# Routing weights computed earlier in the round, and a residual sum moved from GpSimd to VectorE, in a graph-attention and expert-network kernel

## The reference

```python
x = x + gnn0(layernorm(x), adj)      # masked softmax attention, then ELU
x = x + ffn0(layernorm(x), ...)      # router picks 2 of 6 experts per node
x = x + gnn1(layernorm(x), adj)      # masked softmax attention, then ELU
x = x + ...                          # one choice of 2 of 8 experts per graph, layernorm
# inside ffn0, per node:
rh = relu(features @ router_w1 + router_b1)
expert_logits = softmax(rh @ router_w2 + router_b2)
top_w, top_i = top_k(expert_logits, 2)
routing_weights = softmax(top_w)
```

## Time and profile before

| | |
|---|---|
| Time, median of 3 runs | 764.93 us (764.13 to 765.67) |
| Time of the profiled execution | 764.48 us |
| Its span | 762.7 us |
| Instructions | 15258 |
| TensorE busy | 607.0 us (80%) |
| VectorE busy | 448.5 us (59%) |
| ScalarE busy | 408.3 us (54%) |
| GpSimd busy | 253.4 us (33%) |

### The profile page before, as it was taken

One profiled execution on the slowest core, in us unless ns is written; L12 is line 12 of the kernel. 1 busy time (PEld: TensorE's weight loads), 2 busy tenths in 40 slices (PEclk: granted clock), 3 DMA queues, 4 the chain that ended last, 5 costly groups with the idle time before them and its releaser, 6 DMA issues.

```text
span 762.7 us, 15258 instructions
## 1 busy us (share of the span) xinstructions
PE 607.0 (80%) x3969; PEld 489.7 (64%) x4001; DVE 448.5 (59%) x1632; ACT 408.3 (54%) x974; POOL 253.4 (33%) x477
## 2 busy tenths in 40 slices
PE   3358779797887978879797797968942699999993
PEld 2236566575665756657575575746631599999993
DVE  3356576686866768677576766765533144444445
ACT  1234455664755658456575665746641255555552
POOL 4312222341423324233232423322221034444444
PEclk9999999998998999899899989999955699999997
DMA  7304214034040320404214041121100454444421
GB/s 155 104 2 125 85 41 126 28 99 119 8 124 11 113 99 26 124 1 124 74 51 124 0 124 46 38 84 30 57 0 0 133 146 139 140 142 142 142 69 55
DMA packets 74598, 61.99 MB, mean 81 GB/s; under 512 B 7772, under 2 KB 62268, under 8 KB 74562
## 3 DMA queue, kind: packets, MB, share of 16 engines
q1 hardware_dynamic: 61344, 56.14, 24.6%
q10 hardware_dynamic: 13218, 5.42, 2.8%
HBM read 57.13 MB, written 4.41 MB: 81 GB/s over the span
## 4 chain that ended last, share of the span: by engine, by line
PE 65%; DVE 12%; ACT 9%; issue 8%; POOL 4%; DMA 1%; ACTq 0%; DVEq 0%; POOLq 0%; SPq 0%
PE bank L1297 13%; PE bank L1310 9%; PE bank L1474 4%; PE wide L240 4%; PE bank L1487 4%; PE wide L207 4%; PE wide L1487 4%; PE wide L1474 3%; DVE at_lk L300 3%; PE bank L1289 3%; PE bank L1290 3%; PE bank L1291 3%; PE wide L232 2%; ACT h L787 2%; ACT h L782 2%
## 5 line engine op out<-in xcount | busy, mean ns | idle before, releaser
L782 ACT ACTIVATE h<-bank,b 128x512 f32<-128x512 f32 x96 | 65.9, 687 | 125.6 <-PE bank L1297 125.3
L1297 PE MATMUL bank<-h,w 128*128 128x512 f32 x192 | 114.3, 680 | 5.1 <-ACT h L787 5.1
L1310 PE MATMUL bank<-w,h2w 128*128 128x128 f32 x768 | 109.6, 288 | 0.0
L1310 PEld LDWEIGHTS bank<-w,h2w 128*128 128x128 f32 x768 | 102.6, 204 | 4.3 <-issue 1.0
L996 DVE TENSOR_TENSOR h2w<-h,wide_w 128x512 f32<-128x512 f32 x96 | 65.6, 683 | 44.3 <-ACT h L782 43.3
L787 ACT ACTIVATE h<-bank,b 128x512 f32<-128x512 f32 x96 | 65.4, 681 | 41.4 <-PE bank L1291 41.2
L1289 PE MATMUL bank<-xnTh,w1h 128*128 128x512 f32 x96 | 76.6, 798 | 0.0
L1316 PE MATMUL wide<-ident,wgt 128*88 128x128 f32 x16 | 6.3, 393 | 72.7 <-DVE wgt L1053 72.7
L324 POOL TENSOR_TENSOR at_src<-at_wh,zero 128x8 bf16<-128x8 f32 x32 | 9.0, 280 | 128.9 <-DVE at_wh L292 128.9
L1316 PEld LDWEIGHTS wide<-ident,wgt 128*88 128x88 f32 x16 | 2.2, 138 | 76.6 <-DVE wgt L1053 76.6
L101 POOL TENSOR_TENSOR at_var_eps<-at_mean_var,eps 128x4 f32<-128x4 f32 x32 | 12.3, 385 | 108.0 <-DVE at_mean_var L94 108.0
(11 more groups left out here) (233 smaller groups left out, 1526.5 us busy)
## 6 DMA issues: line engine op xcount, KB each, us to landing
wide_w<-w_scratch SPq DMA_DIRECT2D x96, 256.0 KB, 4.3
mask<-in_L_ffn_W SPq DMA_DIRECT2D x128, 128.0 KB, 2.1
x<-in_x SPq DMA_DIRECT2D x16, 256.0 KB, 5.9
xin<-in_x SPq DMA_DIRECT2D x16, 256.0 KB, 6.0
adj_in<-in_adj SPq DMA_DIRECT2D x16, 256.0 KB, 6.3
out<-at_pr ACTq DMA_DIRECT2D x8, 256.0 KB, 3.0
out<-at_prT ACTq DMA_DIRECT2D x8, 256.0 KB, 2.7
W<-in_L_ffn_W SPq DMA_DIRECT2D x2, 512.0 KB
```

The costliest lines, as they stand in the source:

```text
L782: a.activation(h2[:, e % 2, :], b_h2[:, :], ACT.Relu, bias=b2[:, e:e + 1]).then_inc(h2_ready, 1)
L1297: pe.matmul(b_h2[:, :], w2[:, e, :], h1[:, e % 2, :], start=True, stop=True).then_inc(l2_done, 1)
L1310: last = pe.matmul(b_out[:, s], h2w[:, e % 2, s], w3[:, e, :], start=False, stop=(e == E0 - 1), skip_group_check=True)
```

## The change

Two things are moved and one changes its engine. The exponential `pq` goes, on ScalarE, from behind the second attention's score copy to a place ahead of `norm_apply_act`. `route_weights` goes, on VectorE, from behind `measure(rn)` to a place ahead of `attn_dve_elu(at0)`; `weight_rows`, its neighbour so far, stays. The residual sum of the first attention is taken from GpSimd and is done by VectorE right behind that ELU, as one operation on 128x512 elements of fp32, both inputs in SBUF. No transfer and no matrix product moves.

```diff
--- before.py
+++ after.py
@@ gpsimd @@
-                if live("attn0", i0):
-                    attn_pool_residual(at0, p, x, x[:, cols(i + 2)], const_ready, i + 2)
@@ scalar @@
                 if attn1:
                     attn_act_rows(at1, a, i - 1)
+                if route:
+                    a.wait_ge(route_step, ROUTE * (i + 1) + 7)
+                    a.activation(pq[:, :, :], pd[:, :, :], ACT.Exp).then_inc(pq_ready, 1)
                 if pool and not last(i0):
...
                     attn_act_z(at1, a, i - 1)
-                if route:
-                    a.wait_ge(route_step, ROUTE * (i + 1) + 7)
-                    a.activation(pq[:, :, :], pd[:, :, :], ACT.Exp).then_inc(pq_ready, 1)
@@ vector @@
                     weigh(n + 3, i, 3)
+                if route:
+                    route_weights(i + 1)
                 if attn0:
                     attn_dve_elu(at0, v, i + 2)
+                    settle(v, const_ready)
+                    v.wait_ge(at0["elu_ready"], i + 3)
+                    v.tensor_tensor(x[:, cols(i + 2)], x[:, cols(i + 2)], at0["prT"][:, :], ALU.add)\
+                        .then_inc(at0["x_ready"], 1)
                 if run:
                     weigh(n + 4, i, 4)
...
                 if route:
-                    route_weights(i + 1)
                     weight_rows(i + 1)
```

## The result

The changed kernel took 671.4 us, the median of 4 runs (668.54 to 673.78), against 765.3 us (764.13 to 766.58) for the kernel before: a ratio of 0.877, with an interval of 0.873 to 0.881. The prediction said 669.0 us. The execution in the trace took 673.78 us and is the slowest of the four. The prediction's sum, worked out from the profiled execution of the kernel before, was 668.4 us, so this execution lies 5.4 us above it.

What follows compares the result with a forecast made beforehand. TensorE was taken to set the pace, stopped once a round by VectorE's `wgt`. Twelve rounds gave 76.6 us, with the other rounds 96.1, off 764.5: 668.4, so 669 us; range 659 to 688, the forecast's own 663 to 675.

Steps and rivals of the forecast that it cites:

- The wait and its place: TensorE's 4.66 us wait for `wgt` ahead of the weights' transpose goes entirely, with 1.4 us to spare.
- The clock: On TensorE behind the wait, the granted clock of 0.52 goes; it and what hangs on it give 1.7 us per round.
- the rival that only the wait goes: TensorE still stands somewhere long enough for the slow clock; 1.5 us in 13 rounds come back, 688 us, chance 0.05.
- L300 and the residual: On VectorE the residual costs 0.69 us plus 0.05 of wait, while L300 falls from 1.75 to 0.69 us.
- What is late next: The exponential L269 on ScalarE becomes the close second; TensorE stands 0.1 to 0.4 us for it, round 25.83 us.
- the term of 76.6 us: The gain in the loop: 12 rounds, each shorter by 6.38 us.
- The terms for round 0 (5.7 us): Round 0 gains 4.42 us of wait and some 1.3 us of clock.
- what lies behind the 12 rounds (8.0): Gains of 6.2 us in round 13's second half and 1.8 us in round 14.
- The transfers: VectorE waits about 0.5 us for `x`, absorbed by 0.74 us of later idle time; nothing charged, upper bound 0.47 us.
- the loop of transfers binds: Rival: the loop from `wrow` through loads, `x`, statistics and weighings limits the rounds; 675 us, or 687, chance 0.14.
- a wait of over 0.5 us per round at `x`: Sign named beforehand: such a wait, at `x` or at `wide_w`, would make the forecast number too low.
- The prologue and round 0: Round -1 gains 5.0 us of wait without clock; round -2 gains 0.8 us from the residual moving to VectorE.

Runs made afterwards that it cites:

- e6: The changed kernel with the exponential `pq` back at its old place on ScalarE, VectorE's new order kept: 702.2 us, ratio 0.918.
- e2: The changed kernel with the first attention's residual given back to GpSimd, only the weights staying moved: 675.5 us, ratio 0.881.
- e7: The kernel before, with 36 unread transposes of a constant put on TensorE ahead of the weights' transpose: 742.3 us, ratio 0.969.
- e1: The changed kernel run again as it is, against the kernel before: 670.0 us, ratio 0.874.
- e3: The changed kernel with each load of `x` issued one group earlier, ahead of the weights' loads: 668.2 us, ratio 0.872.
- e4: The changed kernel with `weight_rows` moved right behind the fifth weighing, ahead of the second attention's maximum and the statistics: 667.6 us, ratio 0.870.
- e8: The changed kernel with both `x` loaded one group ahead and the weights' rows copied early: 667.1 us, ratio 0.871.
- e5: The kernel before with only the residual moved to VectorE, both orders of the weights as they were: 758.4 us, ratio 0.991.

## Why the prediction was right, and which terms were off

**The wait and its place: right.** TensorE has no idle time left ahead of L1319 in any round, and `wgt` is 1.40 us early (predicted 1.4). e6 shows that `pq`'s move is needed for it, e2 that these two moves make nearly all of the gain: 766 to 675 us.

**The clock: right.** I charged 1.7 us per round to it, and e7 measured 1.7 with L1316 starting as late in its round as before. Over the whole kernel that is 23 us (765.6 to 742.3), a quarter of the change's gain. It came with the wait's end, as the window at 1.00 shows, so the rival that only the wait goes is out.

**L300 and the residual: right.** L300 went from 1.75 to 0.69 us. In the prediction the residual and the faster L300 about paid for each other on VectorE, and they did. The Trainium skill ("SBUF — State Buffer", section "SBUF: two separate sides"), by which a VectorE operation with two SBUF inputs is blocked beside a GpSimd operation that reads SBUF, is borne out by e2: L300 at 1.77 us beside a residual of 1.49 us. The residual did wait 0.21 us for its own ELU in the round shown, where 0.05 had been put.

**What is late next: right.** L269 is what TensorE waits for, 0.29 us (predicted 0.1 to 0.4). Counted from L1319 (311.47, predicted at 336.17), L300 starts 0.32 us later than predicted (312.59 against 336.97). The rounds came at 26.00 and 25.87 us against 25.83, so the term of 76.6 us measured 74.6 and 76.1. The terms for round 0 (5.7 us) and for what lies behind the 12 rounds (8.0) measured 5.3 and 8.3, and 5.5 and 8.3 in e1.

**The transfers: a term too small, its absorption right.** I gave the wait for `x` 0.47 us. It is 1.30 us in the round shown, and 11.0 us in 11 waits in e1:

```profile
DVE at_stats L88 <- DMA x<-in_x: 11.0, 11, 2.3
```

e3 took this away and the rounds got shorter by 0.18 us. So I sized the wait at half of what it was, but the idle time behind it took four fifths of it, and the rival "the loop of transfers binds" (675 us) did not come. What is wrong by it is 2 us in all, and only by traces. The prediction had named a wait of over 0.5 us per round at `x` as a sign that its number is too low; the wait is there, but it is worth no more than this. It also shows how little a share of the chain says: the loads of `x` had 12% of the span in it, and with the wait gone the median is 1.8 us lower, within the scatter.

**The prologue and round 0: the term that was mis-sized.** The prediction took 5.0 us for round -1 and 0.8 us for round -2 before round 0's mark, 5.8 us, and said of the weights that they "are needed no more tightly". That is true in the loop and false in round 0. In the kernel before, the first weighing of round 0 waited for ScalarE alone:

```profile
64.65 0.69 DVE L996 TENSOR_TENSOR h2w<-h,wide_w 128x512 f32<-128x512 f32 x1 [0.37 <-ACT h L782]
```

In the changed kernel it stood 4.24 us for `wide_w`, and 3.01 us in e1. TensorE then waited for it too, here in the first trace and then in e1:

```profile
64.22 1.98 PE L1313 MATMUL bank<-w,h2w 128*128 128x128 f32 x8 [2.04 <-DVE h2w L994]
```

```profile
62.28 1.16 PE L1313 MATMUL bank<-w,h2w 128*128 128x128 f32 x8 [0.86 <-DVE h2w L994]
```

The term measured 2.45 us in the first trace and 5.5 in e1. Of the 3.1 us between them, 1.9 are there when L1313 starts. In e1 the store was issued 0.7 us earlier (55.87), and its six loads took 2.71 us to issue against 4.17; from the store to the first load passed 2.3 us in the first trace and 2.2 in e1 (1.4 in e4), which doesn't part the two. Why the issue took longer isn't shown. The other 1.1 us comes behind L1313, where the granted clock was 0.57 over 4 us of the first trace and 1.00 over the same 4 us of e1:

```profile
64.00:68.00 4.00, 3.79 (x14) 2.94 (x14) 2.65 (x5) 0.00 (x0) 0.00 (x0) 0.57 0.98 293
```

```profile
64.00:68.00 4.00, 3.38 (x22) 2.68 (x20) 2.21 (x7) 2.98 (x7) 0.00 (x0) 1.00 0.89 265
```

So behind a stall of 2.04 us the slow clock was back, where the prediction had a clock of 1.00 through the rounds. The 40 slices of the page are too coarse to show it.

In the traces in which the clock held there, the term is 4.8 us (e3) and 5.5 (e1) with the weights late, 5.7 (e4) and 6.4 (e8) with the weights early. The 5.8 us of the prediction lies among them. What it left out is how far the transfers scatter in the one round in which no earlier group covers them. That it is so close is partly luck. By e2's mark, 73.11, the weights alone gave 3.9 us of the 5.0, and the residual 1.6 (73.11 to 71.48) where 0.8 had been put; each is one trace, in a place that scatters.

The same may be why runs with the late weights lie further apart, 3.5 us in e1 and in e3, than those with the early ones, 1.9 in e4 and 1.7 in e8. I did not take more traces to show it run by run.

**What is left.** The version with the row of weights early (e4, 667.6 us) beats both kernels. It is ahead of the change by some 0.4% (ratio 0.870 [0.869, 0.872] against 0.874 [0.872, 0.876]), a difference just clear of the scatter.

## What to carry to other kernels

When an engine waits for one small result, list what stands ahead of its producer on the producer's engine: each instruction that isn't its input can go behind, if whatever the result itself needs is moved with it. A wait of TensorE long enough to lower its clock costs more than its length, and the row behind the wait, not the wait, shows how much. When a round gets shorter, go through what it used to cover, in the first round as well as in the loop: the first one has no earlier work to hide a transfer, and behind one stall there the slow clock was back.

## What the runs showed of the hardware beyond what was expected

**A small GpSimd operation beside a VectorE one.** `route_var_eps`, 128x4, took 0.20 us in the kernel before. Now, from its timeline on GpSimd:

```profile
315.33 0.75 POOL L101 TENSOR_TENSOR route_var_eps<-route_mean_var,eps 128x4 f32<-128x4 f32 x1 [7.25 <-DVE route_mean_var L94]
```

VectorE's timeline has the copy of the row and then a weighing beside it:

```profile
315.17 0.26 DVE L1061 COPY wrow<-wide 88x128 f32<-88x128 f32 x1
315.34 0.68 DVE L994 TENSOR_TENSOR h2w<-h,wide_w 128x512 f32<-128x512 f32 x1
```

The weighing starts 0.01 us after it and ends at 316.02, the small addition at 316.08, as if it had stood until the weighing was over. This fits the same port rule, with GpSimd as the one that waits. It isn't shown: by the records the addition began first, and no run takes away the weighing alone. The median of this instruction is 0.20 us in e5, whose order of the weights is the old one, and 0.75 us in e2, e6 and the change, which share the new one. VectorE then stands 0.64 us for `route_rstd`, about as much as the addition is longer, 0.55.

**Filling a wait.** 36 small fp32 transposes, recorded with 272 ns each, kept the granted clock at 1.00 behind a place where TensorE had stood 4.66 us and the clock had then been 0.52, and the kernel with more work was 3% faster.
